# Two fused attention layers: one ring of three PSUM pairs in the first, a causal mask added inside the maximum in the second

## The reference

```python
# first attention: 16 heads of 64, no mask
q = z @ wq @ fcq_w + fcq_b; k = z @ wk @ fck_w + fck_b; v = z @ wv @ fcv_w + fcv_b
scores = einsum('bihd,bjhd->bhij', q, k) / sqrt(64)
out = einsum('bhij,bjhd->bihd', softmax(scores), v).reshape(b, n, 1024) @ fco_w + fco_b

# second attention: 16 heads of 8, a rotary part of 32 shared by the heads, causal
c_kv = x @ W_kv_down
k_rope = rotary(c_kv @ W_k_rope); q_rope = rotary(x @ W_q_rope)
k = c_kv @ W_k_up; v = c_kv @ W_v_up; q = x @ W_q
scores = (q k^T + q_rope k_rope^T) / sqrt(40)
scores = where(triu(ones, k=1), -inf, scores)          # key later than query
attn = softmax(scores) @ v @ W_o
```

## Time and profile before

| | |
|---|---|
| median of three runs | 1772.4 us |
| the profiled execution: its own time, its span | 1763.42 us, 1761.4 us |
| mean granted TensorE clock | 0.922 |
| busy: PE, DVE, ACT, POOL | 1505.1, 987.9, 829.0, 821.8 us |
| first attention | about 79 to 848 us |
| second attention with its prologue | about 994 to 1453 us |

### The profile page before, as it was taken

One profiled execution on the slowest core, in us unless ns is written; L12 is line 12 of the kernel. 1 busy time (PEld: TensorE's weight loads), 2 busy tenths in 40 slices (PEclk: granted clock), 3 DMA queues, 4 the chain that ended last, 5 costly groups with the idle time before them and its releaser, 6 DMA issues. The chain is left out here.

```text
span 1761.4 us, 20151 instructions
## 1 busy us (share of the span) xinstructions
PE 1505.1 (85%) x6830; PEld 853.1 (48%) x6830; DVE 987.9 (56%) x1328; ACT 829.0 (47%) x1408; POOL 821.8 (47%) x447
## 2 busy tenths in 40 slices
PE   4679999999999999998448756998989995399998
PEld 3534444444444444443336425665655653277776
DVE  3265666666666665661535565554554513498887
ACT  2224444444444444444215341555545563287887
POOL 0227777777777777777215322223332002054444
PEclk9679999999999999999569887998999996599999
DMA  3000000000000000000144122011111102412200
GB/s 77 4 1 1 14 14 13 13 14 13 14 13 13 14 13 14 13 13 13 48 97 95 48 61 59 20 25 36 51 41 25 25 1 110 75 23 48 60 6 6
DMA packets 34565, 54.94 MB, mean 31 GB/s; under 512 B 10009, under 2 KB 15650, under 8 KB 33762
## 3 DMA queue, kind: packets, MB, share of 16 engines
q1 hardware_dynamic: 34482, 53.87, 12.4%
HBM read 37.34 MB, written 1.44 MB: 22 GB/s over the span
## 5 line engine op out<-in xcount | busy, mean ns | idle before, releaser
L480 POOL TENSOR_TENSOR psum_k<-psum_k,prob 128x1024 f32<-128x1024 f32 x192 | 456.4, 2399 | 99.7 <-ACT prob L523 99.7
L523 ACT ACTIVATE prob<-st 128x512 f32<-128x512 f32 x512 | 278.3, 596 | 408.4 <-PE st L661 407.9
L544 DVE TENSOR_REDUCE mx<-work 128x2 f32<-128x1024 f32 x256 | 312.5, 1226 | 105.8 <-PE work L606 104.9
L631 PE MATMUL pv<-prob,c_all 128*64 128x512 f32 x1024 | 257.6, 609 | 0.0
L659 PE MATMUL st<-qq,ak 128*128 128x512 f32 x512 | 233.9, 457 | 13.1 <-ACT prob L523 8.9
L1488 ACT ACTIVATE l_prob<-l_banks 128x1024 f32<-128x1024 f32 (+7 forms) x256 | 160.5, 652 | 166.8 <-PE l_banks L1612 114.0
L661 PE MATMUL st<-q,kb 128*128 128x512 f32 x512 | 202.9, 396 | 0.0
L1759 POOL TENSOR_TENSOR silu_rest<-silu,silu_lead 128x512 fp32r<-128x512 f32 x72 | 113.0, 1569 | 149.1 <-ACT silu_lead L1803 149.1
L1565 DVE TENSOR_REDUCE l_mx<-l_banks 128x1 f32<-128x640 f32 (+3 forms) x128 | 129.9, 1024 | 86.6 <-PE l_banks L1595 85.7
L659 PEld LDWEIGHTS st<-qq,ak 128*128 128x128 f32 x512 | 96.3, 188 | 126.7 <-issue 58.6
L1831 DVE TENSOR_TENSOR silu<-silu,gb 128x512 f32<-128x512 f32 x128 | 139.3, 1090 | 27.3 <-ACT silu L1810 25.3
(11 more groups left out here) (228 smaller groups left out, 2527.6 us busy)
## 6 DMA issues: line engine op xcount, KB each, us to landing
gb<-scratch_gates SPq DMA_DIRECT2D x8, 2048.0 KB, 14.0
rb<-scratch_sums SPq DMA_DIRECT2D x32, 256.0 KB
l_qq<-qr SPq DMA_DIRECT2D x8, 768.0 KB, 5.7
whole_r<-in_w SPq DMA_DIRECT2D x2, 2304.0 KB, 11.8
l_kk<-l_head SPq DMA_DIRECT2D x64, 64.0 KB, 2.0
l_qq<-l_head SPq DMA_DIRECT2D x64, 64.0 KB, 2.0
x<-in_x SPq DMA_DIRECT2D x4, 256.0 KB, 6.5
whole_r<-in_up SPq DMA_DIRECT2D x1, 1024.0 KB, 5.4
```

The lines of the kernel that those rows point to most:

```text
L480: nc.gpsimd.tensor_tensor(total[:, h, :], total[:, h, :], prob[kt % 4][:, h, :], ALU.add).then_inc(summed, 1)
L523: nc.scalar.activation(prob[kt % 4][:, h, ts(j, BLK)], st[h][:, :], ACT.Exp, scale=D0 ** -0.5).then_inc(exp_done, 1)
L544: nc.vector.reduce_max(mx[:, x % 2, :, x // 2], buf[:, :, :], AX.X).then_inc(read, 1)
L631: ins = nc.tensor.matmul(pv[D0 * h:D0 * (h + 1), ts(j, BLK)], m.c_all[:, TT * (s // PAIRS) + kt, :], prob[kt % 4][:, h, ts(j, BLK)], start ...
```

## The change

First attention: `GAPS` becomes `AFTER_SCORES` and `AFTER_VALUES`. Both `ST` of a key tile stand together, then up to two units, then both `PV`, then the rest. `st` and `work` become three pairs of banks, taken in turn by every `ST` (both heads) and every unit; each waits for the reader of the tile three places earlier. One exponential of 128x1024 replaces two of 128x512, so whoever waited for one head's now waits for both. `s` waits for ScalarE's copy of its queries (`hi_done`), and no longer for VectorE's read of `q`.

Second attention: the mask pass in `score` goes. VectorE adds a row of a 128x1024 mask in SBUF (`m.causal`, zeros, with the triangle in the last 128 columns) and takes the maximum in one instruction, one per head, that writes the sums back to PSUM. The pass in the transposed scores stays. The two smallest `e` take one bank. The planner's costs and ranks change, and its conditions for `ST` and `PV`. The prologue loads `causal` (512 KB), and a mask tile of 64 KB in place of 128 KB.

```diff
-GAPS = {
-    (0, 0): [("q", 0)], (0, 1): [("q", 1)],
-    (1, 0): [("s", 0)], (1, 1): [("s", 1)], (1, 3): [("s", 2)],
-    (2, 0): [("s", 3)], (2, 1): [("l", 0)], (2, 2): [("s", 4)], (2, 3): [("s", 5)],
-    (3, 0): [("s", 6)], (3, 1): [("s", 7)], (3, 3): [("s", 8), ("r", 0)],
-    (4, 0): [("s", 9)], (4, 1): [("s", 10)], (4, 2): [("s", 11)], (4, 3): [("s", 12)],
-    (5, 0): [("s", 13)], (5, 1): [("s", 14)], (5, 2): [("s", 15)], (5, 3): [("n", 0)],
-    (6, 1): [("m", 0)], (6, 3): [("g", 0)],
+AFTER_SCORES = {
+    0: [("q", 0), ("q", 1)],
+    1: [("s", 0), ("s", 1)], 2: [("s", 3), ("s", 4)], 3: [("s", 6), ("s", 7)], 4: [("s", 9), ("s", 10)],
+    5: [("s", 12), ("s", 13)], 6: [("s", 15)],
+}
+AFTER_VALUES = {
+    1: [("s", 2), ("l", 0)], 2: [("s", 5)], 3: [("s", 8), ("r", 0)], 4: [("s", 11), ("n", 0)], 5: [("s", 14), ("g", 0)],
+    6: [("m", 0)],
 }
...
-        st = [ctx.enter_context(nc.psum_tensor(f"st{h}", [P, BLK], F32)) for h in R2]
-        work = [ctx.enter_context(nc.psum_tensor(f"work{h}", [P, 2, BLK], F32)) for h in R2]
+        pair = [ctx.enter_context(nc.psum_tensor(f"pair{i}", [P, 2, BLK], F32)) for i in range(RING)]
+        tiles = ring_of_pairs()
+        turn = {tile: i for i, tile in enumerate(tiles)}
+        def buffer(kind, at):
+            return pair[turn[(kind, at)] % RING]
+        def await_buffer(pe, kind, at):
+            i = turn[(kind, at)]
+            if i >= RING:
+                before, count = tiles[i - RING]
+                pe.wait_ge(exp_done if before == "ST" else read, count + 1)
...
-                            nc.scalar.activation(prob[kt % 4][:, h, ts(j, BLK)], st[h][:, :], ACT.Exp,
-                                                 scale=D0 ** -0.5).then_inc(exp_done, 1)
+                        nc.scalar.activation(prob[kt % 4][:, :, ts(j, BLK)], buffer("ST", at)[:, :, :], ACT.Exp,
+                                             scale=D0 ** -0.5).then_inc(exp_done, 1)
...
-            for dst, src in ((wkv, d["wkv"]), (wv, d["wv1"]), (m.coef, d["coef"])):
+            for dst, src in ((wkv, d["wkv"]), (wv, d["wv1"]), (m.coef, d["coef"]), (m.causal, d["causal"]),
+                             (masks, d["masks"])):
...
+def pass_time(width):
+    return max(0.2, 0.24 * width / BLK)
 def pe_time(item):
     if kind == "ST":
-        return 0.07 + 0.235 * (T - P * item[2]) / BLK
+        return 0.2 + sum(pass_time(hi - lo) for lo, hi in q_pieces(item[2]))
-    if kind in "es":
-        return (2 if kind == "e" else 1) * (0.07 + 0.235 * s_width(item[2]) / BLK)
+    if kind == "e":
+        return 2 * pass_time(s_width(item[2]))
+    if kind == "s":
+        return pass_time(BLK) + pass_time(s_width(item[2]) - BLK)
...
+    if kind == "e":
+        return 1 if 2 * s_width(item[2]) <= BLK else 2
...
-                rank = {"PV": 1.0, "k": 0.0, "q": 0.0}.get(q[0][0], waiting)
-                found.append((start + rank * 0.3, len(found), start, q, banks))
+                rank = {"PV": 1.5, "k": 0.6, "q": 0.6}.get(q[0][0], waiting)
+                found.append((start + rank * 0.1, len(found), start, q, banks))
...
-                if kind == "e":
-                    nc.vector.reduce_max(mx[:, 2 * x:2 * x + 2, t], ...)
-                elif kind == "s":
-                    nc.vector.reduce_max(mx[:, g, t:t + 1], buf[:, 0:s_width(t)], AX.X).then_inc(read, 1)
+                if kind in "es":
+                    t = item[2]
+                    hidden = m.causal[:, T - s_width(t):T]
+                    parts = [(item[3], buf)] if kind == "s" else list(zip((2 * item[3], 2 * item[3] + 1), halves_of(item)))
+                    for g, scores in parts:
+                        ins = nc.vector.tensor_tensor_reduce(scores[:, 0:s_width(t)], scores[:, 0:s_width(t)], hidden, 1.0,
+                                                             -3e38, ALU.add, ALU.max, mx[:, g, t:t + 1])
+                    ins.then_inc(read, 1)
...
             def score(out, k, g, t, width):
-                return nc.tensor.matmul(out[:, width - P:width], m.identr[:, :], m.maskr[:, 0, :], start=False, stop=True)
+                for lo in range(0, width, BLK):
+                    end = min(width, lo + BLK)
+                    ins = nc.tensor.matmul(out[:, lo:end], qq[k % 2][:, g, ts(t, P)], kk[k % 2][:, g, lo:end],
+                                           start=True, stop=True)
+                return ins
```

More of the change, by code:

```diff
@@ L325, in step_script @@
     for kt in range(TT):
[L326 to L329, removed]
+        out += [("ST", kt, 0), ("ST", kt, 1)]
+        out += [("UNIT",) + u for u in AFTER_SCORES.get(kt, []) if u in has]
+        if kt or n:
+            out += [("PV", kt - 1, 0), ("PV", kt - 1, 1)]
+        out += [("UNIT",) + u for u in AFTER_VALUES.get(kt, []) if u in has]
     return out
@@ L354, in place, with ring_of_pairs @@
     return first_of(n) + in_psum(step_order(n)).index(unit)
+RING = 3
+def ring_of_pairs():
+    tiles = [("UNIT", u) for u in range(len(in_psum(FIRST_UNITS)))]
+    for n in range(STEPS0):
+        for what, *rest in step_script(n):
+            if what == "ST":
+                tiles.append(("ST", 2 * TT * n + 2 * rest[0] + rest[1]))
+            elif what == "UNIT" and rest[0] not in "rn":
+                tiles.append(("UNIT", place(n, tuple(rest))))
+    last = first_of(STEPS0)
+    return tiles + [("UNIT", last), ("UNIT", last + 1)]
 LAST_UNITS = [("l", 0), ("r", 0), ("n", 0), ("g", 0)]
@@ L585, in unit @@
             def unit(kind, x, u, k):
[L586 to L589 removed]
+                buf = buffer("UNIT", u)
+                await_buffer(pe, "UNIT", u)
                 if kind == "q":
@@ L600, in unit @@
                     if half == 0 and t % TPB == 0:
-                        pe.wait_ge(read, place(k - 1, ("q", t // TPB)) + 1)
+                        pe.wait_ge(hi_done, 4 * k + 2 * (t // TPB) + 2)
                     keys = ds(batch(k) + BLK * half, BLK)
@@ L1165, in _ @@
             copy_xt(0)
-            act.wait_ge(loaded, 16 * 8)
+            act.wait_ge(loaded, 16 * 9)
             for j in range(NBLK):
@@ L1184, in _ @@
             transpose_block(nc, pe, m, 0, tr, xn_ready, xt_ready, transposed)
-            pe.wait_ge(loaded, 16 * 8)
+            pe.wait_ge(loaded, 16 * 9)
             for j in range(NBLK):
@@ L1254, in read_time @@
     if kind in "es":
-        return 0.15 + (2 if kind == "e" else 1) * s_width(item[2]) / 960
+        return (2 if kind == "e" else 1) * (0.16 + s_width(item[2]) / 960)
     return {"k": 1.4, "q": 1.4, "m": 0.3, "t": 0.8, "PV": 0.0}[kind]
@@ L1281, in ready @@
         if kind == "ST":
-            need = [("row", n, item[3] // 2)] + [("PV", n, item[2] - 2, 0)] * (item[2] >= 2)
-            need += [("PV", n - 1, TT - 2, 0)] * (n > 0 and item[2] == 0) + [("PV", n - 1, TT - 1, 0)] * (n > 0 and item[2] == 1)
+            back = TT * n + item[2] - 2
+            need = [("row", n, item[3] // 2)]
+            need += [("PV", back // TT, back % TT, len(q_pieces(back % TT)) - 1)] * (back >= 0)
         elif kind == "PV":
-            need = [("ST", n, item[2], g) for g in range(4)] + [("ut", n - 1)] * (n > 0)
+            need = [("ST", n, item[2], 3)] + [("ut", n - 1)] * (n > 0)
         elif kind in "es":
@@ L1397, in buffer, with halves_of @@
             return banks[b // 2][:, BLK * (b % 2):BLK * (b % 2) + BLK * banks_of(item)]
+        def halves_of(item):
+            size = BLK * banks_of(item) // 2
+            return [buffer(item)[:, ts(h, size)] for h in range(2)]
         def score_at(n, kt, g):
@@ L1614, in transposed_scores @@
                     if x == 0:
-                        ins = nc.tensor.matmul(buf[:, at:at + P], m.identr[:, :], m.maskr[:, 1, :], start=False, stop=True)
+                        ins = nc.tensor.matmul(buf[:, at:at + P], m.identr[:, :], m.maskr[:, :], start=False, stop=True)
                 ins.then_inc(st_filled, 1)
@@ L1628, in unit @@
                 if kind == "e":
-                    for h in R2:
-                        ins = score(buf[:, ts(h, BLK)], k, 2 * item[3] + h, item[2], s_width(item[2]))
+                    for h, out in enumerate(halves_of(item)):
+                        ins = score(out, k, 2 * item[3] + h, item[2], s_width(item[2]))
                 elif kind == "s":
```

76 lines of the change are left out of this document (34 added, 42 removed).

## The result

The changed kernel took 1767.55 us (median of 20 runs, 1764.09 to 1772.43), the kernel before 1772.3 us (20 runs, 1764.82 to 1776.94): ratio 0.9975, 95% interval 0.9964 to 0.9986. The forecast was -20 us; it came to -5. The time lies 1.5 us above the forecast's own range (1730 to 1766) and inside the wide one (1708 to 1790).

What follows compares the result with a forecast made beforehand. TensorE was taken to bound both attentions, with DVE fuller in the second's entry. First attention -10, mask -15, entry +3, prologue +2 sum to -20, from the median 1772.4 to 1752 us; own range 1730 to 1766, wide range 1708 to 1790.

Steps and rivals of the forecast that it cites:

- The small `e` in one bank and the planner's conditions: Second attention: sharing a bank and the planner's new conditions were set at 0, having no measured row.
- 0 and 23: Second attention: bounds in us on the gain from mask passes removed from `score` beyond the entry; two thirds, -15, taken.
- Rival D: Second attention hangs on loads and order, not on the maxima: 0 in place of -15, total 1767 us; chance 0.22.
- -15 + 3: Second attention: 15 us gained by dropping mask passes, 3 us lost in the entry to DVE's longer instructions.
- The entry: Start of the second attention, only maxima made, DVE 6.5 of 8 us busy: new maximum instructions cost +3 us.
- The long maximum: Second attention, DVE: mask add and maximum in one instruction takes 1.2 to 1.4 us for 1024, no bound.
- Rival A: Second attention: new maximum runs at half rate, DVE becomes the bound; +45 in total, 1817 us; chance 0.10.
- `on`: First attention: falls inside GpSimd's second add of key tile 4, waits about 1.6 us; `g` then waits 0.2 us.
- the loss: First attention: waits for `mmax` (1.5 us), the row of maxima (0.5) and `g` (0.2) cost 2.2 us per step.
- `s s`: First attention: two `s` in a row, five times a step, save 0.14 us each, 0.70; bounds 0 and 0.20 each.
- rivals B: First attention: `mmax` waits for both GpSimd adds, another 2.35 us per step; total +15, 1787 us; chance 0.10.
- C: First attention: `mmax` comes before the first add, both waits vanish, 30 us more gained, 1722 us; chance 0.15.

Runs made afterwards that it cites:

- e2: The changed kernel with the second attention's planner costs, ranks, conditions and banks of before, mask still added in the maximum: 1746.7 us, ratio 0.985 to before.
- e3: The changed kernel with its new planner and order, but the mask pass on TensorE and plain maxima of before: 1793.8 us, ratio 1.0123 to before.
- e1: The kernel before with only the first attention changed: 1753.6 us, ratio 0.9899 to before.
- e4: The changed kernel with one number changed, the planner's time from a head buffer's release to its reload 8.0 us, not 3.0: 1711.1 us, ratio 0.9658 to before.
- e6: The changed kernel with the planner's time from a head buffer's release to its reload 12.0 us, not 3.0: 1696.3 us, ratio 0.9577 to before.
- e10: The changed kernel with planner release time 12.0, `s` 15 behind `s` 14, `m` ahead of both `PV`, only 128 columns of `causal` loaded: 1692.5 us, ratio 0.9546 to before.

## Why the prediction was wrong

**Where it failed: the second attention.** The step that failed is "The small `e` in one bank and the planner's conditions have no row of their own; I set them at 0, within the bounds above", together with its bounds, "0 and 23". The prediction named the new order as something the loads depend on, then gave it no price and no loss side. It cost 28.3 us with the new operations by the stages (e2 against after), 21 by the medians; what it did is to leave 2.6 to 3.5 us of work beside reloads that take 6.5 us or more, so that TensorE waited 47.5 us for them, and the clock fell with it. The row that should have warned stands in the waits of the kernel before: `l_qq<-l_head` 47.3 us in 12 waits. I read one window in which TensorE idled 1.3 of 44 us and took it for the stage; further on, from 1216 to 1304, it was busy 35.95 and 36.73 of 44. Rival D, "the second attention does not hang on the maxima but on the loads and the order", had the right place, at 0 for a price of +21.

**What the mask was worth**: -15 + 3 = -12 forecast, -13.5 measured by the stage under the order of before, -20.5 where the loads are covered, -27.2 under the new order (there the clock, 0.86 and 0.87, is low in both); by the medians of the kernels -10, -15 and -26. Right in kind and near in size.

**The entry**, +3 forecast, went the other way: from the clearing of `pv` to the first `ST`, 1091.1 - 1038.3 = 52.8 before and 1072.8 - 1022.9 = 49.9 after. It is 49.7 with the old planner as well (e2) and 52.8 with the old operations under the new one (e3), so the operations did it. DVE is at 6.68 of 8 us there, fuller than the 6.5 of before. Why it still ends sooner (one head per instruction, so a shorter wait before it, would fit) no run separates.

**The long maximum**: 1.238 + 0.141 = 1.38 us for 1024 (forecast 1.2 to 1.4). Rival A, half rate, is refuted: (1238 - 720)/512 = 1.01 ns per element. The two groups of DVE, by shape for the first:

```profile
L1601 DVE CUSTOM_DVE_ANT_0 l_banks<-l_banks,causal 128x1024 f32<-128x1024 f32 x32 | 39.6, 1238 | 20.0 <-PE l_banks L1630 19.6
L1601 DVE DVE_READ_ACCUMULATOR2_ANT l_mx<- 128x1 f32 x256 | 36.2, 141 | 0.0
...
L1601 DVE CUSTOM_DVE_ANT_0 l_banks<-l_banks,causal 128x512 f32<-128x512 f32 x32 | 21.6, 720 | 5.9 <-PE l_banks L1630 5.9
```

Here the rule of the Trainium skill, VectorE: DVE Perf Modes, section Two Vector instructions with no wait between them, was right: the accumulator is read by an instruction of its own, 0.141 us each. What followed from it for the entry was wrong all the same. In the price of rival A, the 20.5 and 1.4 us per 44 us are its 19.2 and the 1.3 us per step, scaled from a step of about 41 us to the window of 44, which the prediction does not say.

**The first attention**: the mechanisms named were right but for `on`; the loss was put too large. Per step, TensorE's time from start to start less its idle time, before and after: `ST` 18.25 and 16.72, `s` 6.84 and 6.15, `PV` 15.38 and 15.10, the wait for an exponential 0.44 and 0. The gain is 1.53 + 0.69 + 0.28 + 0.44 = 2.94 us, against 2.9 forecast. `s s` gave 0.14 each, as taken from `PV`; the full 0.20, which the prediction had set beside the rule of the Trainium skill, TensorEngine Tiling (Array Packing), section Key Properties, would have given 1.0 in place of 0.69. The loss was put at 2.2 and is 1.5 to 1.7: a step went from 45.6 to 44.0 us. The step after, around `m`:

```profile
406.87 0.49 PE L631 MATMUL pair<-kb,qq 64*128 64x512 f32 x1
407.30 1.94 PE L656 MATMUL pv<-prob,c_all 128*64 128x512 f32 x8
410.60 0.38 PE L635 MATMUL pair<-ident,mmax 128*16 128x128 f32 x2 [1.36 <-DVE mmax L575]
...
412.97 1.94 PE L656 MATMUL pv<-prob,c_all 128*64 128x512 f32 x8
415.00 0.50 PE L683 MATMUL pair<-qq,ak 128*128 128x512 f32 x1
```

`m` waits 1.36 us (1.5 forecast) and `mmax` takes 1.78, so rivals B (2.35 us more) and C (no wait) are refuted. But the row of maxima lands almost in time: 415.00 - 410.60 = 4.40 from `m` to the first `ST`. The two `PV` ahead of that `ST` take 415.00 - 412.97 = 2.03 here, where 1.86 is their time without a wait, so 0.17 of waiting (0 to 0.24 over the steps) where 0.5 was forecast. The 4.78 of the earlier trace rows was the price of another place: there SP's first issue came 1.05 us after `m` (104.97), here 0.80 (411.40). `g` starts 0.59 after the `s` ahead of it, whose own time is 0.43: 0.16 of waiting, near the 0.2. So an undisturbed step is 43.9 to 44.1 us, not 44.9. Thirteen steps between like points took 592.9 us before and 576.6 after, although one of them took 48.2; the other 3 us of the 19.4 came at both ends.

That one step shows a wait that the prediction did not have. `n` now stands in key tile 4, and there `on` waits for the DMA that brings the sums' reciprocals, 1.25 us in an ordinary step and 3.13 in this one; in the same step before the change, with `n` in key tile 5, it waited for nothing. The maxima behind it start late, and `g` waits for them:

```profile
534.37 2.24 DVE L591 TENSOR_TENSOR on<-ut,rb 128x1024 f32<-128x1024 f32 x1 [3.13 <-DMA rb<-scratch_sums]
...
537.80 1.73 PE L645 MATMUL pair<-on,g_all 128*128 128x512 f32 x3 [2.78 <-DVE mx L571]
```

The same 2.8 us of TensorE's time stand in this step of e1, e2, e4 and e6; in e1 it took 46.7 us at a clock of 1.00. The rest of the 48.2 goes with the clock, 0.94 from 540 to 560. Why the DMA is late in this step no run shows.

**The prologue**: +2 forecast, +2.9 measured, wait 4.11 for 1.92 (about 4 forecast); e10 confirms the cause.

**The signs named in advance**: DVE (26 of 44, under 34) held. A step of the first attention sits on the lower edge of its 44.0 to 45.5: the median of the thirteen is 43.99, and seven of them are below 44.0, by up to 0.08. "If TensorE idles there by more than it did before plus 8 us" is the one that struck: +31.5 over the stage. The 256 matmuls are gone (6830 to 6574).

**In the sum**: -10 (was -19), -15 + 3 (was +21), +2 (was +3). Two errors of opposite sign, -9 and +33, hid part of each other. That the time came so near the forecast's own range, and inside the wide one, is luck.

## What to carry to other kernels

An order that a planner writes is a part of the change with a price of its own: where edits touch its figures, compare the two orders at each place where a buffer is released and reused, and give the term a loss side. For every reload under double buffering measure release to first use once (here 6.5 us, eight DMA issues and a landing, and over 8 us where the issues were slow) and put it, not a guess, into the plan; read the waits over the whole stage, never from one good window. A wait that recurs every few tens of microseconds is to be priced at more than its length, since TensorE's granted clock fell where such waits stood (0.87 against 0.95). And where a difference is under 10 us, set the medians of the kernels beside the stages of their profiles.

## What the runs showed of the hardware

- TensorE lost more than it waited: e4 took away 41.3 us of idle time, and 20.7 us of busy time went with it, at the same 1,951 or 1,952 matmuls, as the mean clock rose from 0.87 to 0.95. By the medians the whole gain was 56 us and not 62, so it is a third to a half as much again.
- The same stage with the same instructions and the same waits took 413.7 us at 0.93 (before) and 420.1 at 0.91 (e1). A stage of this kernel is thus known only to some 6 us from a single profile; what the clock followed there stays open.
- `tensor_tensor_reduce` reads and writes PSUM at 1.01 ns per element (720 ns for 512, 1238 for 1024), about the rate of a plain reduction (1.04), and pays 0.141 us for the accumulator.
- A reload of eight DMAs on one queue took 6.5 us from first issue to first use, or 8.1 to 8.5 where its first four issues took 4.0 to 4.4 us in place of 2.4 (after, seven and four of eleven reloads).
- `ak,qq` and `kb,qq` of 64 rows start together, and a second such pair follows after 0.34 us (422.84, 423.18, 423.53 in the trace after), where a lone one took 0.43.
